# Token centring by two half-array matmuls, gate temporaries in SBUF, and a new order of the expert stage

## The reference, cut to what matters

```python
t = _to_tokens(x)                       # (16, 3600, 64): a token has 64 channels
x_n = _ln_t(t)                          # centre and scale each token over its 64 channels
router_probs = softmax(x_n @ router_w + router_b)          # 8 experts
top_p, top_i = top_k(router_probs, 2)
top_p = top_p / sum(top_p)
expert_out = einsum('bnd,edc->bnec', x_n, expert_w) + expert_b
t = t + einsum('bnk,bnkc->bnc', top_p, take_along_axis(expert_out, top_i, axis=2))
```

## Time and profile before

| what | us |
|---|---|
| median of 3 runs | 1518.93 (1518.44 to 1519.48) |
| the profiled execution, its own time | 1521.44 |
| its span, first to last instruction | 1519.7 |
| expert stage: first `tokens` to the end | 919.8 to 1519.7 |
| one region, from `add_out` at 1201.10 to the one at 1233.62 | 32.52 |
| mean granted TensorE clock | 0.988 of full speed |

### The profile page before, as it was taken

One profiled execution on the slowest core, in us unless ns is written; L12 is line 12 of the kernel. 1 busy time (PEld: TensorE's weight loads), 2 busy tenths in 40 slices (PEclk: granted clock), 3 DMA queues, 4 the chain that ended last, 5 costly groups with the idle time before them and its releaser, 6 DMA issues.

```text
span 1519.7 us, 30382 instructions
## 1 busy us (share of the span) xinstructions
PE 1351.9 (89%) x9344; PEld 1181.8 (78%) x9344; DVE 842.6 (55%) x1786; ACT 708.9 (47%) x2313; POOL 630.5 (41%) x752
## 2 busy tenths in 40 slices
PE   7899999999998999999999997777777777777777
PEld 5899999999998999999999995445555445555544
DVE  4788888555552222222222225667776667776666
ACT  5567766334342222220000004666666666667664
POOL 2566665000000000003444444666666666666666
PEclk9999999999999999999999997999999999999999
DMA  4111111000000000001121110000001000000001
GB/s 135 44 65 47 61 65 61 1 0 0 0 0 0 0 0 0 0 0 39 58 77 59 58 58 1 22 23 23 22 24 42 22 22 22 22 30 36 23 23 44
DMA packets 15372, 46.68 MB, mean 31 GB/s; under 512 B 2912, under 2 KB 2912, under 8 KB 15328
## 3 DMA queue, kind: packets, MB, share of 16 engines
q1 hardware_dynamic: 15184, 45.76, 8.5%
q10 hardware_dynamic: 144, 0.33, 0.1%
HBM read 31.33 MB, written 14.75 MB: 30 GB/s over the span
## 4 chain that ended last, share of the span: by engine, by line
PE 75%; DVE 11%; issue 7%; ACT 4%; DVEq 1%; POOL 1%; DMA 0%; ACTq 0%; POOLq 0%
PE twin L954 30%; PE twin L871 24%; PE twin L1010 8%; PE twin L1022 5%; DVE parts L733 3%; PE twin L991 3%; PE twin L977 2%; PE twin L862 2%; PE twin L856 2%; DVE scratch L793 1%; DVE stat L725 1%; DVE act_buf L801 1%; ACT more L506 1%; ACT late L506 1%; DVE late L793 1%
## 5 line engine op out<-in xcount | busy, mean ns | idle before, releaser
L954 PE MATMUL twin<-kbuf,late 128*128 128x136 f32 (+2 forms) x3940 | 458.1, 280 | 5.0 <-DVE kbuf L701 5.0
L954 PEld LDWEIGHTS twin<-kbuf,late 128*128 128x128 f32 x3940 | 457.9, 192 | 5.3 <-DVE kbuf L701 5.3
L871 PE MATMUL twin<-parts 128*128 128x384 f32 (+2 forms) x2070 | 393.8, 342 | 0.0
L871 PEld LDWEIGHTS twin<-parts 128*128 128x128 f32 x2070 | 372.5, 189 | 2.9 <-issue 2.5
L297 POOL TENSOR_TENSOR act_buf<-kbuf,x_in 128x144 f32 (+1 forms) x198 | 96.6, 488 | 564.7 <-DVE kbuf L707 564.7
L707 DVE SCALAR_TENSOR_TENSOR kbuf<-twin,act_buf 128x144 f32<-128x144 f32 x394 | 121.3, 308 | 337.1 <-PE twin L954 337.1
L1010 PE MATMUL twin<-em,parts 64*128 64x512 f32 x1404 | 228.7, 431 | 2.8 <-DVE scratch L793 2.8
L322 POOL TENSOR_TENSOR scratch<-scratch 128x512 f32<-128x512 f32 x126 | 160.8, 1276 | 112.4 <-ACT scratch L506 73.5
L473 ACT ACTIVATE x_in<-twin 128x384 f32<-128x384 f32 (+1 forms) x90 | 42.0, 467 | 336.0 <-PE twin L977 336.0
L793 DVE TENSOR_TENSOR scratch<-twin,scratch 128x512 f32<-128x512 f32 (+1 forms) x126 | 115.5, 917 | 95.0 <-PE twin L1010 91.1
L1010 PEld LDWEIGHTS twin<-em,parts 64*128 64x128 f32 x1404 | 115.1, 187 | 52.8 <-issue 38.9
(11 more groups left out here) (102 smaller groups left out, 1585.2 us busy)
## 6 DMA issues: line engine op xcount, KB each, us to landing
x_in<-x SPq DMA_DIRECT2D x36, 400.0 KB, 3.6
x_in<-x_col SPq DMA_DIRECT2D x20, 720.0 KB, 4.1
result<-act_buf SPq DMA_DIRECT2D x36, 400.0 KB, 2.8
scratch<-L_conv_w_d ACTq DMA_DIRECT2D x1, 320.0 KB, 4.7
scratch<-L_conv_w_u SPq DMA_DIRECT2D x1, 320.0 KB, 6.0
late<-L_conv_w_r SPq DMA_DIRECT2D x1, 320.0 KB, 6.3
late<-L_conv_w_l SPq DMA_DIRECT2D x1, 320.0 KB, 7.0
ew<-L_ffn_expert_w SPq DMA_DIRECT2D x2, 128.0 KB, 6.2
```

The lines of the kernel that those rows point to most:

```text
L871: last = mm(acc[:, lo:hi], vw[:, k, wpart, si], carry[:, cpart, g, lo + s * BG:hi + s * BG], start=first and si == 0, stop=final and si == ...
L954: last = mm(banks[CONV[g]][:, lo * BG:hi * BG], hw[:, k, si], kbuf[:, g, lo + s:hi + s].rearrange("p j b -> p (j b)"), start=si == 0, stop ...
```

## The change

- `tokens`: for each tile two matmuls on 64 rows with 72 moving columns (64 centred channels and 8 logits of one half), one into each bank of `twin[2]` (banks 4 and 5). `cl_w` becomes [128, 72]: each half's centring block and router weights; the centring matrix gets a tensor of its own.
- `copy_tokens` reads both banks; the copy is now two ACT instructions (the logits, then the tokens), so three in all.
- `channels` writes to bank 6 instead of 5. The softmax temporaries go from bank 6 to `sq` in SBUF (a tensor the first stage used), the bias row to an SBUF tensor of its own.
- `ACT_TILES` changes from (2, 4, 5, 6, 7, 8, 9, 10) to (6, 7, 8, 9, 10, 11, 12); DVE gates both halves of tiles 0 to 5.
- New order in the three `region()` loops: `channels`, `first_part` and `second_part` of chunk c run at tile c + 5 (they ran at c + 3, c + 3 and c + 4), with `channels` ahead of `tokens` on PE; ACT takes `first_part`, `copy_tokens`, `gate_odd`, `inv_std_tokens` in this order, the last one tile earlier; DVE takes `square_sums` ahead of the gate; softmax step 0 stands at tile 6, and steps 7 and 8 at tile 9.
- In the fill, `tokens` uses the pairs 2, 0, 1, 2, 0 and `channels` banks 6 and 7.

```diff
@@ -31,7 +31,8 @@
     TC = 3
     NCK = -(-TILES // TC)
     TOKS = TILES * TN
-    CLW = P + 2 * E
+    HW = C + E
+    CLW = 2 * HW
     BIG = 1.0e30
     ctx = ExitStack()
...
@@ -88,8 +89,8 @@
         rstd = sb("rstd", [P, 2, NC])
         ident = sb("ident", [P, P])
         mean_w = sb("mean_w", [P, P])
-        cl_w = sb("cl_w", [P, CLW])
-        center_w = cl_w[:, 0:P]
+        cl_w = sb("cl_w", [P, HW])
+        center_w = sb("center_w", [P, P])
         mean_r = sb("mean_r", [P, P], F32R)
         center_r = sb("center_r", [P, P], F32R)
         eps_c = sb("eps_c", [P, 3])
...
@@ -107,12 +108,11 @@
         CEN, VAR = [2, 3], [4, 5]
         CEN0, VAR0 = [2, 3, 6, 7], [4, 5]
         FRONT = CH + 2
-        CT, TB = 4, 5
-        LOG, SUM = 6, 7
+        CTS, TB, SUM = 2, 6, 7
         PREP = [6, 7]
-        FILL_CT, FILL_TB = [4, 0, 1, 2, 3], [5, 7, 5, 7, 5]
-
-        ACT_TILES = (2, 4, 5, 6, 7, 8, 9, 10)
+        FILL_CT, FILL_TB = [2, 0, 1, 2, 0], [6, 7, 6, 7, 6]
+
+        ACT_TILES = (6, 7, 8, 9, 10, 11, 12)
         TERMS = [(0, 0), (0, 1), (1, 0)]
         LAG = 2
         SEQ = 2 * TILES
...
@@ -152,7 +152,7 @@
         GAP_STEP = 8
         EX_STEP = 12
-        STEP_AT = [(7, 0), (7, 1), (7, 2), (8, 0), (8, 1), (8, 2), (9, 0), (9, 1), (9, 2), (10, 0), (10, 1), (10, 2),
+        STEP_AT = [(6, 2), (7, 0), (7, 1), (7, 2), (8, 0), (8, 1), (8, 2), (9, 0), (9, 2), (10, 0), (10, 1), (10, 2),
                    (11, 0), (11, 1), (11, 2), (12, 0), (12, 1)]
         EXP_TILE = STEP_AT[GAP_STEP - 1][0] + 1
...
@@ -462,16 +462,17 @@
                 copy_back(u, u)
-            def copy_tokens(j, slot, c, bank=CT):
+            def copy_tokens(j, slot, c, pair=CTS):
                 n, b, k = NCK * j + c, (slot + c) % 2, len(tiles_of(c))
-                src = banks[bank][:, 0:TC * CLW].rearrange("p (t n) -> p t n", t=TC)[:, 0:k]
+                src = twin[pair][:, :, 0:k * HW].rearrange("p q (t n) -> p t q n", n=HW)
                 act.wait_ge(s_ct, n + 1)
                 if later(n - 1):
                     act.wait_ge(s_vr, n - 1)
                 if later(j):
                     act.wait_ge(s_tb, n - NCK + 1)
-                act.activation(sqt[:, b, 0:k], src[:, :, 0:P], ACT.Square).then_inc(s_sq2, 1)
-                act.activation(tl[:, c, 0:k], src, ACT.Copy).then_inc(s_cp, 1)
+                act.activation(sqt[:, b, 0:k].rearrange("p t (q c) -> p t q c", q=2), src[:, :, :, 0:C], ACT.Square).then_inc(s_sq2, 1)
+                act.activation(tl[:, c, 0:k, P:].rearrange("p t (q e) -> p t q e", q=2), src[:, :, :, C:], ACT.Copy)
+                act.activation(tl[:, c, 0:k, 0:P].rearrange("p t (q c) -> p t q c", q=2), src[:, :, :, 0:C], ACT.Copy).then_inc(s_cp, 1)
             def inv_std_tokens(j, slot, c):
                 n, b, k = NCK * j + c, (slot + c) % 2, len(tiles_of(c))
...
@@ -513,15 +514,14 @@
                     if now is not None:
                         if p == EXP_TILE:
                             exponential(now)
-                        if 2 <= p < NCK + 2:
-                            inv_std_tokens(now, 1 - slot, p - 2)
+                        if 5 <= p < NCK + 5:
+                            first_part(now, 1 - slot, p - 5)
+                        if p < NCK:
+                            copy_tokens(now, 1 - slot, p)
                     if p in ACT_TILES:
                         gate_odd(j, slot, p)
-                    if now is not None:
-                        if p < NCK:
-                            copy_tokens(now, 1 - slot, p)
-                        if 3 <= p < NCK + 3:
-                            first_part(now, 1 - slot, p - 3)
+                    if now is not None and 1 <= p < NCK + 1:
+                        inv_std_tokens(now, 1 - slot, p - 1)
             for c in range(NCK + 2):
                 if c < NCK:
...
@@ -634,14 +634,16 @@
             nc.vector.tensor_tensor(ew[:, E * C:], ew[:, E * C:], banks[PREP[1]][:, 0:E], ALU.subtract).then_inc(s_em, 1)
             dve.wait_ge(s_em, 2)
             nc.vector.scalar_tensor_tensor(ew[:, 0:E * C], eb[:, 0:E * C], 1.0 / C, ew[:, 0:E * C], ALU.mult, ALU.add).then_inc(s_em, 1)
-            nc.vector.memset(cl_w[:, P:], 0.0).then_inc(s_em, 1)
-            dve.wait_ge(s_em, 4)
+            for q in range(2):
+                half = slice(q * C, (q + 1) * C)
+                nc.vector.tensor_copy(cl_w[half, 0:C], center_w[half, half]).then_inc(s_em, 1)
+            dve.wait_ge(s_em, 5)
             nc.vector.tensor_copy(em[:, 0], ew[:, 0:E * C]).then_inc(s_em, 1)
             for q in range(2):
                 half = slice(q * C, (q + 1) * C)
-                nc.vector.tensor_copy(cl_w[half, P + q * E:P + (q + 1) * E], ew[half, E * C:]).then_inc(s_em, 1)
-            nc.vector.tensor_copy(bias_row, eb[:, E * C:]).then_inc(s_em, 1)
-            dve.wait_ge(s_em, 8)
+                nc.vector.tensor_copy(cl_w[half, C:], ew[half, E * C:]).then_inc(s_em, 1)
+            nc.vector.tensor_copy(bias_row[:, :], eb[:, E * C:]).then_inc(s_em, 1)
+            dve.wait_ge(s_em, 9)
             nc.vector.tensor_tensor(em[:, 1], ew[:, 0:E * C], em[:, 0].bitcast(F32), ALU.subtract).then_inc(s_em, 1)
             with dve.Fori(1, (HP - 2) // 2) as i:
                 for u in range(2):
...
@@ -737,8 +739,9 @@
                 return v.unsqueeze(2).to_broadcast([P, NG, E])
             gap, ex, inv = (best[:, k] for k in range(3))
-            work = banks[LOG][:, 0:2 * NSM].rearrange("p (k n e) -> p k n e", k=2, e=E)
-            small = banks[LOG][:, 2 * NSM:2 * NSM + 3 * NG].rearrange("p (k n) -> p k n", k=3)
+            spare = sq[:, :, :].rearrange("p b n -> p (b n)")
+            work = spare[:, 0:2 * NSM].rearrange("p (k n e) -> p k n e", k=2, e=E)
+            small = spare[:, 2 * NSM:2 * NSM + 3 * NG].rearrange("p (k n) -> p k n", k=3)
             m1, idx, den = (small[:, k] for k in range(3))
             def softmax_steps(j, slot):
...
@@ -746,7 +749,7 @@
                 v = nc.vector
                 return [
-                    lambda: v.tensor_tensor(logit, raw_logit, bias_row.unsqueeze(1).to_broadcast([P, NG, E]), ALU.add),
+                    lambda: v.tensor_tensor(logit, raw_logit, bias_row[:, :].unsqueeze(1).to_broadcast([P, NG, E]), ALU.add),
                     lambda: v.tensor_reduce(m1, logit, AX.X, ALU.max),
                     lambda: v.tensor_tensor(work[:, 0], logit, spread(m1), ALU.subtract),
                     lambda: v.scalar_tensor_tensor(hit, work[:, 0], 0.0, rank_w[:, :, :], ALU.is_equal, ALU.mult),
...
@@ -812,14 +815,12 @@
             def region(j, slot, now):
                 for p in range(TILES):
+                    if now is not None and 1 <= p < NCK + 1:
+                        square_sums(now, 1 - slot, p - 1)
+                    gate_tile(j, slot, p)
+                    if now is not None and 5 <= p < NCK + 5:
+                        second_part(now, 1 - slot, p - 5)
                     for part in range(3):
-                        if part == 0:
-                            gate_tile(j, slot, p)
-                            if now is not None:
-                                if 1 <= p < NCK + 1:
-                                    square_sums(now, 1 - slot, p - 1)
-                                if 4 <= p < NCK + 4:
-                                    second_part(now, 1 - slot, p - 4)
                         if part == 2:
                             add_behind(j, p)
                         if now is not None:
...
@@ -966,16 +967,17 @@
             def tile_lo(p):
                 return min(p * TN, REG - TN)
-            def tokens(j, slot, c, bank=CT):
+            def tokens(j, slot, c, pair=CTS, behind=1):
                 n = NCK * j + c
-                if later(n):
-                    if bank == CT:
-                        pe.wait_ge(s_cp, n)
+                if later(n - behind + 1):
+                    pe.wait_ge(s_cp, n - behind + 1)
                 flat = cols[:, j].rearrange("p g w b -> p (g w b)")
                 for i, p in enumerate(tiles_of(c)):
-                    last = mm(banks[bank][:, CLW * i:CLW * (i + 1)], flat[:, tile_lo(p):tile_lo(p) + TN], cl_w[:, :],
-                              start=True, stop=True)
+                    for q in range(2):
+                        half = slice(q * C, (q + 1) * C)
+                        last = mm(twin[pair][:, q, HW * i:HW * (i + 1)], flat[half, tile_lo(p):tile_lo(p) + TN], cl_w[half, :],
+                                  start=True, stop=True)
                 last.then_inc(s_ct, 1)
             def channels(j, slot, c, bank=TB):
...
@@ -1027,20 +1029,20 @@
                 for p in range(TILES):
                     experts(j, slot, p)
                     if now is not None:
+                        if 5 <= p < NCK + 5:
+                            channels(now, 1 - slot, p - 5)
                         if p < NCK:
                             tokens(now, 1 - slot, p)
```

(8 more changed lines are left out.)

## The result

| | median us | lowest to highest | runs |
|---|---|---|---|
| before | 1519.40 | 1518.44 to 1521.43 | 7 |
| changed | 1505.38 | 1503.82 to 1513.01 | 7 |

The ratio is 0.9918, 95% interval 0.9895 to 0.9940: 14 us faster. The time lies inside the range of 1450 to 1528, but the gain is only a little over half of the 25 that was forecast (1494). The profiled execution took 1505.38, its span is 1503.6.

A forecast was written before the change was run, and what follows sets the result against it. No engine is full; PE waits for DVE's `second_part`, 5.5 us of each 32.52 us region. The new loop, 14.4 + 16.3 = 30.7 plus 0.3, gives 31.0, saving 25.5 us over 17 regions: 1494, range 1450 to 1528.

The forecast's parts named there:

- the four stalls: PE's `channels` waiting for DVE's `second_part`: four stalls of some 1.5 us would go, up to 5.5 a region.
- The loop of the walk: Dependencies closing over one expert-stage region: 14.4 us from `gate_tile(0)` to POOL's last scaling, then 11.9, together 26.3 without contention.
- the 27.0: Region length without contention, raised from 26.3 for ACT's seven back-to-back gates (12.2 us) behind four first parts.
- seven blocked: Softmax steps on DVE held up by POOL's pair sums in tiles 6 to 12, costing 4.4 us a region.
- the walk's 30.7 to 31.0: Region length with contention: 14.4 + 16.3 = 30.7, plus 0.3 for hand-offs, 31.0 against 32.5.
- a granted clock of 1.00: PE's clock in the expert-stage region, read as 1.00 (2.4 GHz); no change of it was priced.
- 0.84 a chunk: PE time of a chunk's half-array `tokens`, taken between 0.42 and 1.68 us.
- Rival C: Half-array matmuls run one after another on PE, 1.68 us a chunk, regions of 33.0, time 1527; chance 0.18.
- The copy, DVE's sixth gate: ACT's third copy instruction, 1.0 us a region, and DVE's gate, 0.53 in tiles 0 to 5: both hidden.
- A: DVE and POOL do not hold each other up in softmax steps: region 27.0 to 27.3, time 1429; chance 0.10.
- B: Only POOL pays for the hold with DVE, at most 2.9 us: region 28.5 to 29, time 1454; chance 0.16.
- D: No change to speak of: seven blocked steps each cost 0.2 us more, loop 32.4, time 1519; chance 0.06.

The follow-up runs named there:

- exp. 1: Kernel before with the new order alone (region loops, ACT_TILES, STEP_AT), old tokens, temporaries in PSUM: 1409.71 us, ratio 0.9276.
- exp. 5: Kernel before with new order, temporaries in SBUF, 144-column tokens and eight filler matmuls ahead of the sum of tile 12: 1463.71 us, ratio 0.9629.
- exp. 6: Changed kernel with two filler matmuls behind each chunk's half-array tokens, none in the wait of tile 1: 1472.25 us, ratio 0.9689 to before.
- experiment 9: New order alone with ScalarE's copy of a chunk split into two instructions, 144-column tokens: 1410.41 us, ratio 0.9280 to before.

## Why the prediction was wrong

By the medians the change comes apart like this:

| part | from, to | us |
|---|---|---|
| the order | 1519.4, 1409.7 (exp. 1) | -109.7 |
| temporaries in SBUF, clock held up | 1409.7, 1463.7 (exp. 5) | +54.0 |
| half-array form, clock held up, with other fillers | 1463.7, 1472.3 (exp. 6) | +8.5 |
| the clock | 1472.3, 1505.4 | +33.1 |

- *The order.* Right in mechanism: the four stalls of the earlier trace rows are gone. The loop of the walk, 26.3, holds: in experiment 1 its first half (from `gate_tile(0)` to step 0) takes 14.3 to 14.4 against 14.4, and its second 11.6 to 11.7 against 11.9, together 26.0. (The terms listed for the second half add up to 13.4, with the two short steps to some 13.2, and not to 11.9; a step ahead of a gate in fact takes 0.28 to 0.29 and not 0.41.) Mis-sized is the 27.0 that it was raised to for ACT's gates in a row.
- *Temporaries in SBUF.* Right in mechanism and in the price of one blocked step, mis-sized in their number: seven blocked, 4.4 us, were counted; four are, 3.1. The walk let step 0 start together with pair sum 6 and every tile's steps meet its pair sum. In the trace the steps of tiles 7 and 8 fall between two pair sums, while POOL waits 0.7 to 0.8 us for ACT's gate of 1.75, and only those from tile 10 on meet one. The second half, put at 16.3, takes 15.1 in experiment 6, and the walk's 30.7 to 31.0 stands against 29.4 at full clock.
- *The step that failed* is the silent one in "a granted clock of 1.00": that PE keeps it. The walk even noted that PE would have "several us to spare", and gave that no price. PE stops for 2.2 us in tile 1 and then runs at 0.50 for 7 or 14 us. So it is PE, and not POOL as the walk has it, that sets the pace of the first half: 16.1 us in two regions and 18.6 in the third, against the 14.4 of the walk and the 14.3 of experiment 6. That costs 33 us. It took away more than the too high 31.0 had hidden: the two errors, 1.6 us a region one way and on average 2.2 the other, leave most of the 11 us by which the forecast was off. That the time still lies within the forecast's own 1478 to 1512 is luck, not a sum that came out.
- *Half-array matmuls.* 0.84 a chunk was assumed; at full clock PE goes from `experts` of tile 0 (L1012 at 1215.92) to the sum at 1217.44 in 1.52. Less the 0.90 from the start of `experts` to what follows, that is 0.62 for the chunk against 0.84 in the earlier trace rows. Rival C is refuted: the halves do run side by side. The 0.2 saved a chunk did not show in the time: at full clock experiment 6 is 8.5 us slower than experiment 5, with other fillers. By the Trainium skill (TensorE: Matmul & The Clock Gate, "Part 3: Packing small matmuls — row/col tiling") such halves run at the same time; the trace agrees, with 0.62 against 0.84.
- *The copy, DVE's sixth gate.* Free, as said (experiment 9 for the copy).
- *Rivals A and B.* A is refuted by 4 stretched steps a region. B too: DVE pays, 3.1, and POOL's busy time stays at 21.3. D is not what happened.
- *The end.* The last region took 28.2 us from `add_out` in its tile 1 to the end of the span, 24.7 before: it starts at half clock, with `experts` at 1.65 instead of 0.96. The fill and first region are 5.6 faster.

## What to carry to other kernels

When a temporary moves from PSUM to SBUF, count the VectorE instructions that now have two SBUF inputs and see whether GpSimd runs in the same stretch: here each meeting cost up to 1 us for an instruction of 0.37, and two parts of one change hid each other (-110 and +54). Where TensorE comes to stand still, look at what its clock does afterwards, and at which queued instruction it waits for: here a wait of 2.2 us once a region was followed by 7 or 14 us at 1.2 GHz. And time the parts of a bundled change one at a time; the order alone was the kernel to keep.

## What the runs showed of the hardware that was not expected

- Work added on TensorE made the kernel faster twice: eight fillers in the wait by 21 us, two behind each chunk by 33 us, with the mean clock going from 0.940 to 0.975 and 0.986.
- Falls of the clock came behind stops of PE of 1.5 to 2.6 us, in the old order and the new, with either form of the tokens; waits of up to 1.1 were followed by none.
- After the fall the clock stayed at 0.50 for about 7 us in two regions and almost 14 in the third, with PE busy all the time on half-array tokens, experts and sums; with 144-column tokens it came back in about 3 in most regions. The spread of the changed kernel's runs goes with it: 1503.8 to 1505.7 at clocks of 0.939 to 0.940, 1512.9 and 1513.0 at 0.934 and 0.933.
- The hold between the engines shows as a longer instruction, not as idle time before it: 0.37 becomes 0.86 to 1.36, so that busy time of DVE rose by 3.6 us a region while its work rose by 0.5.
